# A third buffer for the key/value input and a third PSUM bank pair for the attention scores, in a fused attention and feed-forward layer

## What is computed

```python
q_c = rms_norm(x @ wq_down.T, q_norm_w)             # rank 1536
q_nope, q_pe = q_c @ wq_up.T, rope(q_c @ wq_rope.T) # 16 heads of 128 and of 64
kv_c = rms_norm(x @ wkv_down.T, kv_norm_w)          # rank 512
kv_up = kv_c @ wkv_up.T                             # 16 heads: 128 of k_nope, 128 of v
k_rope = rope(x @ wk_rope.T)                        # 64, shared by the heads
scores = einsum(q, k) / sqrt(192)                   # q, k = [nope, rope]
probs = softmax(where(causal, scores, -inf))
x = layernorm(x + einsum(probs, v) @ wo.T)
x = layernorm(x + mlp(x, shared) + mlp(x, routed) * comb_w)
```

## Time and profile before

| | us |
|---|---|
| runs shown: median of 2 | 4487.09 |
| lowest and highest of them | 4428.27, 4545.91 |
| the profiled execution | 4138.27 |
| its span on the slowest core (6) | 4137.0 |
| spans of the 8 cores in it | 4079.4 to 4137.0 |
| busy: TensorE, VectorE, ScalarE, GpSimd | 3084.2, 1453.7, 897.4, 311.4 |
| stage A, B, C, D, E (by the barriers, rounded) | 434, 432, 1212, 282, 1777 |

### The profile page before, as it was taken

How to read it: one execution, slowest core, us unless ns; L and a number is a source line. 1 busy time by engine, 2 the same in 40 slices (tenths; PEclk the granted TensorE clock), 3 DMA queues, 4 the chain that set the end, 5 groups by cost and what they waited for, 6 DMA issues and landing times.

```text
span 4137.0 us, 39429 instructions; the slowest of 8 cores (4079.4 to 4137.0 us)
## 1 busy us (share of the span) xinstructions
PE 3084.2 (75%) x14108; PEld 1343.7 (32%) x14338; DVE 1453.7 (35%) x2079; ACT 897.4 (22%) x1085; POOL 311.4 (8%) x377
## 2 busy tenths in 40 slices
PE   2667244467777778788647369999999999999982
PEld 0223011132333334234223024444444444444430
DVE  2112344445554555554502522121212212122144
ACT  1111011235454544544502100000000000000021
POOL 1001100000000000000010001111111011110100
PEclk9989677786777677667678589999999999999985
DMA  9044622215344353523583256749576495764802
GB/s 131 1 59 62 90 40 34 32 25 102 60 88 77 70 92 59 104 53 55 95 170 36 17 70 58 88 43 102 67 69 80 43 104 70 71 79 44 102 1 81
DMA packets 716975, 281.58 MB, mean 68 GB/s; under 512 B 662257, under 2 KB 695537, under 8 KB 716658
## 3 DMA queue, kind: packets, MB, share of 16 engines
q0 software_dynamic: 405776, 181.69, 37.4%
q1 hardware_dynamic: 311010, 97.35, 11.8%
HBM read 348.99 MB, written 18.87 MB: 89 GB/s over the span
## 4 chain that ended last, share of the span: by engine, by line
PE 61%; DVE 13%; DMA 11%; issue 6%; ACT 5%; another core or an unknown queue 1%; SPq 1%; POOL 0%; DVEq 0%; ACTq 0%; POOLq 0%
PE pdnE L1324 12%; PE puE L1289 11%; PE pgE L1281 11%; DMA Pt<-P 4%; PE pOC L914 4%; PE paC L845 3%; PE pkvB L567 3%; PE paC L779 3%; PE pdD L1087 3%; DVE smx L872 3%; PE paC L841 3%; DMA wuE<-su 2%; PE paC L752 2%; PE pqcA L329 2%
## 5 line engine op out<-in xcount | busy, mean ns | idle before, releaser
L1281 PE MATMUL pgE<-x1b,wgE 128*128 128x512 bf16 x2256 | 523.1, 382 | 28.3 <-DMA wgE<-sg 23.9
L1289 PE MATMUL puE<-x1b,wuE 128*128 128x512 bf16 x2259 | 519.4, 380 | 9.4 <-DMA wuE<-su 7.0
L1324 PE MATMUL pdnE<-O_sb,wdE 128*128 128x512 bf16 x2258 | 504.5, 383 | 26.1 <-issue 23.7
L1300 DVE CAST usE<-puE 128x512 bf16<-128x512 f32 x144 | 99.6, 692 | 856.2 <-ACT gsE L1296 496.4
L1296 ACT ACTIVATE gsE<-pgE 128x512 bf16<-128x512 f32 x144 | 86.0, 597 | 1407.4 <-PE puE L1289 1203.3
L841 PE MATMUL paC<-K,qnC 128*128 128x512 bf16 x544 | 280.5, 516 | 141.1 <-ACT S L858 102.5
L872 DVE TENSOR_REDUCE smx<-S 128x1 f32<-128x4096 f32 (+7 forms) x128 | 326.8, 2553 | 18.4 <-DVE S L865 5.8
L845 PE MATMUL paC<-kr_bf,qpC 64*128 64x512 bf16 x576 | 295.5, 513 | 45.9 <-ACT S L858 26.0
L1324 PEld LDWEIGHTS pdnE<-O_sb,wdE 128*128 128x128 bf16 x2304 | 226.8, 99 | 303.8 <-issue 38.9
L1281 PEld LDWEIGHTS pgE<-x1b,wgE 128*128 128x128 bf16 x2304 | 226.4, 98 | 304.0 <-issue 37.9
L805 ACT ACTIVATE P<-S,smn 128x4096 bf16<-128x4096 f32 (+7 forms) x128 | 283.3, 2213 | 156.2 <-DMA Pt<-P 148.2
(11 more groups left out here) (193 smaller groups left out, 2345.9 us busy)
## 6 DMA issues: line engine op xcount, KB each, us to landing
wgE<-sg POOLq DMA_DIRECT2D x64, 512.0 KB, 8.9
wuE<-su POOLq DMA_DIRECT2D x64, 512.0 KB, 9.4
wdE<-sd POOLq DMA_DIRECT2D x64, 512.0 KB, 16.7
xkB<-xf POOLq DMA_DIRECT2D x8, 2048.0 KB, 15.7
xsum<-xo SPq DMA_DIRECT2D x1, 8192.0 KB, 47.6
woD<-wo POOLq DMA_DIRECT2D x16, 512.0 KB, 6.7
out<-xsum SPq DMA_DIRECT2D x1, 8192.0 KB, 22.0
wqd_sb<-wqd POOLq DMA_DIRECT2D x1, 6144.0 KB, 67.1
```

Source lines behind the costliest of these rows:

```text
L1281: i = ten.matmul(pg[w][:], wg_sl[sl][:, dc * 128:(dc + 1) * 128], x1b[:, dc * TOK + tt * 512: dc * TOK + tt * 512 + 512], start=(dc == 0), ...
L1289: i = ten.matmul(pu[w][:], wu_sl[sl][:, dc * 128:(dc + 1) * 128], x1b[:, dc * TOK + tt * 512: dc * TOK + tt * 512 + 512], start=(dc == 0), ...
L1324: i = ten.matmul(pdn[w][:], wd_sl[dsl][:, oc * 128:(oc + 1) * 128], h_buf[:, ic2 * TOK + tt * 512: ic2 * TOK + tt * 512 + 512], start=(ic2 ...
```

## The change

In stage B a third `xk` tile with its two semaphores: slots are taken modulo 3, three blocks are loaded ahead, and after block kb the load is that of block kb + 3. The tables built there stay those of block kb + 2. In stage C a third `pa` tile with its semaphore: units take the three in turn, and the places that wait for every tile wait for three. PSUM is then full (3 x 2 + 2 banks).

```diff
-            xk = [sbB(f"xkB{i}", [128, NDC * 512], BF16) for i in range(2)]
+            xk = [sbB(f"xkB{i}", [128, NDC * 512], BF16) for i in range(3)]
-            s_xk = [pswd() for i in range(2)]
-            s_xkf = [psem() for i in range(2)]
+            s_xk = [pswd() for i in range(3)]
+            s_xkf = [psem() for i in range(3)]
             def load_xk(kb):
-                sl = kb % 2
+                sl = kb % 3
-            for kb in range(2):
+            for kb in range(3):
                 load_xk(kb)
             for kb in range(8):
-                sl = kb % 2
+                sl = kb % 3
...
                 s_xkf[sl].inc(i)
+                if kb + 3 < 8:
+                    load_xk(kb + 3)
                 if kb + 2 < 8:
-                    load_xk(kb + 2)
                     build_k_tables(kb + 2)
...
-            pa = [psC("paC0"), psC("paC1")]
+            pa = [psC("paC0"), psC("paC1"), psC("paC2")]
-            s_paC = [psem(), psem()]
+            s_paC = [psem(), psem(), psem()]
             def fill_bank():
-                w = _rot[0] % 2
+                w = _rot[0] % 3
...
                     c = t - 1
                     s_paC[0].wait(vec)
                     s_paC[1].wait(vec)
+                    s_paC[2].wait(vec)
                     s_smax.inc(vec.reduce_max(smx[:, c:c + 1],
...
                 vb = (h // 2) % 2
                 s_paC[0].wait(ten)
                 s_paC[1].wait(ten)
+                s_paC[2].wait(ten)
```

## The result

| | before | after |
|---|---|---|
| the profiled execution, us | 4138.27 | 4110.02 |
| median of all runs, us | 4225.49 (10 runs) | 4112.85 (12 runs) |
| ratio after / before, 95% interval | | 0.9923 (0.9905 to 0.9942) |
| key/value stage, start of the first to start of the last matmul with `xk`, mean of 8 cores | 379.9 | 378.3 |
| attention, first K eviction to last matmul of the last PV, mean of 8 cores | 1184.4 | 1153.6 |

The account below looks back on a forecast made before the run. No engine was full, so waits bound the kernel, with TensorE waiting for score and K-build banks. Terms -2.6 - 17.0 - 12.0 - 4.5 + 4 = -32 us (0.77%); 4487.09 x 0.9923 = 4452 us, range 4250 to 4550.

Parts of the forecast that it names:

- The base of the number: Whole kernel: the 0.77% gain applied to 4487.09 us, the median of two runs shown, giving 4452 us.
- Key/value stage, -2.6: Third xk buffer: only block 5's 2.66 us wait for the position row goes; -2.6 us, from -2.6 to +8.
- Odd heads, -17.0: Start of odd heads: a third score unit fills during TensorE's wait; 2.16 us in seven heads, 1.9 in the last.
- K builds, -12.0: K build ahead of seven even heads: a third unit fills during the 4.69 us wait, saving 1.72 us each.
- Rival 2 (the clock rises earlier): K builds and odd heads' S(8), S(7) run at a higher TensorE clock; -76 us, up to -91; chance 0.12.
- Rival 4 (the builds lose the higher clock): TensorE resumes cool through K build, V build, S(8), S(7); about 26 us per head pair, all seven +150; chance 0.07.
- The prediction's sign for it, a lower granted clock from 1163 to 1201: K build, V build and the even head's start: a lower granted clock there would show the forecast wrong.
- Second half, -4.5 and +4 to cancel: S(5)'s third unit stops waiting, about 0.3 us x 15, if transposes don't take it back; added waits cost 4 us.
- The added waits: Satisfied waits ahead of reduce_max, S(8) and PV: 0.05 us each, 0 to 8 us in all, taken as 4.
- Rival 3 (nothing reaches the end): Attention stage: transposes or copies are late instead, so no gain reaches the end; -10 to +18 us; chance 0.19.

Follow-up runs that it names:

- e1: Only the third xk buffer added to the kernel before, score tiles unchanged: ratio 1.0006, key/value stage 377.3 us against 379.9.
- e5: The changed kernel without TensorE's two waits (tiles 0 and 1) ahead of S(8): ratio 0.984 to the kernel before, attention stage 1119.7 us.
- e14: The kernel before, two pa tiles, without the waits ahead of S(8) and with the q load issued later: ratio 0.985, attention stage 1139.7 us.
- e12: The changed kernel, three pa tiles, without the waits ahead of S(8) and with the q load issued later: ratio 0.975 to before, attention stage 1104.2 us.
- e3: Third pa tile used in the K and V builds alone, scores taking turns in two: ratio 1.0012 to the kernel before, attention stage 1188.2 us.
- e10: The kernel before, two pa tiles, with only the q load moved behind S(8) and S(7) of the next head: ratio 0.9936, attention stage 1157.9 us.
- e4: Third pa tile used in the scores alone, builds taking turns in two: ratio 0.9945 to the kernel before, attention stage 1154.4 us.

## Why the prediction was right and wrong

- **The base of the number, wrong.** The step that failed is "I carry the gain over as a share: 4487.09 x 0.9923": it took the two runs shown for the scale, and the lower end of the range, (4138 + 4428)/2 - 32, rests on one of them too. The working itself gave 4106 us on the scale of the profiled execution; that execution now measured 4110.02, and the median of all runs was 4112.85, below the range. The profile's own time was the better scale: its cores agree in the granted clock (0.838 to 0.843), and it lies 290 us below the lower run shown.
- **Key/value stage, -2.6: right.** 379.9 to 378.3; e1, with that edit alone, gave 377.3. TensorE's single wait for `xk` is 13.4 us (13.8 before); the last table's position row stands ahead of its matmul:

```profile
772.24 3.64 PE L590 MATMUL pkrB<-xkB,wkr_sb 128*64 128x512 bf16 x16
775.81 1.04 PE L196 MATMUL ptb<-poskb,ones_r 1*32 1x512 f32 x2
```

- **Odd heads, -17.0: right in kind, 12.4 in size.** The term was one unit, 2.16 us, in every head. It held where the third unit could be full in time: 2.16 in heads 7 and 13 and 1.80 in head 1, which start S(8) ahead of the last mask, 1.76 and 2.15 in heads 9 and 15, but 0.6 to 1.0 in heads 3, 5 and 11. The step that failed is "the stretch from 1243.07 to about 1249.9 holds three units": I kept that stretch while the last exps moved. Before, S(8) started 4.3 to 7.2 us before the last exp ended (means by head); after, 2.9 to 3.2 in heads 3, 5 and 11. The exps gained on the masks in the second half, the wait ahead of S(8) hangs on the last mask, and three units need 6.5 us. e5, without that wait, has the whole 2.1.
- **K builds, -12.0: the build right, the sum wrong.** It measured 2.51 us each, 17.6 in all, more than the one unit of 1.72; with the q load out of the way, where a build with two tiles is shorter already, it is that unit (15.17 in e14, 13.44 in e12). The step that failed is "what follows is TensorE work without a stop, so it moves as a whole": there is a stop, the one ahead of S(8), which the view of before had (17.2 us for the last V evictions), and "in the sum every stretch keeps its level" did not hold behind it. Of 56 even heads 32 ran S(8) and S(7) cool, against 10, and 52 ran at least part of PV at the lower level, against 28. e3 nets nothing of this term.
- **Rival 2 (the clock rises earlier)** did not come: in odd heads the masks of S(8) and S(7) are 7.56 us apart before and after.
- **Rival 4 (the builds lose the higher clock)** was near the mark in what would happen, not where: no K or V build got slower (V evictions from first to last 13.44 before, 13.45 after); the fall comes behind them. The prediction's sign for it, a lower granted clock from 1163 to 1201, came: 0.57 from 1184.52 to 1200.03. The Trainium skill, "TensorE: Matmul & The Clock Gate", section "HAM oscillation — how this bites in real kernels", has waits between bursts let the clock fall. The traces agree that no head without a stop here was cool (24 of 24 after, 56 of 56 in each of e5, e12 and e14), but not that such a stop decides it: of the 56 heads before, all with a stop of 2.1 to 2.3 us, 46 stayed at the higher level.
- **Second half, -4.5 and +4 to cancel: too small.** It measured 1.21 x 8 + 0.93 x 7 = 16.2 us. "If transposes don't take it back" was the right condition, but I saw no transfer that the change would move. It moved the q load from one transpose to another, cheaper one; e10 shows the load's price by moving it out altogether. The added waits were put about right: mask end to reduce_max of S(7) went from 0.10 to 0.17 us (0.05 more was assumed), and TensorE's start of PV behind the mask is 0.1 later.
- **Rival 3 (nothing reaches the end): wrong.** PV still waits for a transpose once, 15.1 us (12.7 in the earlier trace rows). The Trainium skill, same page and section, has another kernel where PSUM double-buffering gave "no further gain"; here the measurement differs: a third tile gives 0.992, and 35 us when the waits around it are gone.

The sum of 32 us against a measured 28 (31.9 on the mean of the spans) owes its closeness to luck, to errors that cancel: the odd heads were put 4.6 us too high, of the K builds' 17.6 us some 15 were given back, and the second halves, put at nothing, brought 16.

**Left open.** Why the same stop ahead of S(8) leads to the lower clock in 10 of 56 heads before and 9 in e4, but in 32 of 32 after and 25 of 32 in e3, where the builds have three tiles. The stop is as long in all of them (2.14 to 2.29 us between the weight loads on either side), and the time that TensorE had worked since its last wait in the K build does not separate the heads either (before: 25.4 to 27.1 us ahead of the cool ones, 25.6 to 27.2 ahead of the others).

## What to carry to other kernels

Take the scale from the execution that was profiled, and don't multiply a share by the median of a few runs that lie far above it and that nothing on record explains. When a buffer is added, read every wait on its set in the diff, one place at a time: where a wait covers only the old members, the rotation decides which work it still catches. And when one engine gets ahead, list what it releases: here the gain of the second halves hung on a load that its progress sends out, and that of the K builds on a two-microsecond stop behind them.

## What the runs showed of the hardware

- A DMA load issued beside a DMA transpose delayed it: the exp that waits for it came 8.47 us after the transpose's issue, 5.15 without the load beside it (e10; 5.08 in the heads of the kernel before that issue no such load); moving the load alone was worth 0.64% (e10).
- After a stop of about 2 us TensorE can run two to eight matmuls at the higher level (0.38 to 0.40 us each) and fall to the lower one (0.61) then, in the midst of work without a gap; behind the same stop, the time from the V build's end to the S(7) mask is then 16.50 us at a granted 0.53 against 11.22 at 1.00 (two heads before). Leaving the waits ahead of S(8) out (e5) took another 34 us from the stage, after the 31 of the change.
- One more wait that was already satisfied, ahead of a VectorE instruction, took 0.07 us: from the end of S(7)'s mask to its reduce_max 0.10 us before, 0.17 after (means of all heads).
